# The second layer of a feed-forward stage as 7 block products instead of 8, with its weight sums made inside the stage

## What is computed

```python
n = layernorm(x3)                                  # rows of 512
h = gelu(n @ proj1.T + proj1_bias)                 # 4096 x 2048, tanh form
out = x3 + tanh(g_ffn) * (h @ proj2.T + proj2_bias)
```

## Time and profile before

| | |
|---|---|
| median of 3 runs | 3560.19 us (3558.64 to 3562.95) |
| the profiled execution | 3558.07 us, its span 3556.3 us |
| mean granted TensorE clock | 0.991 |
| TensorE matmuls, share of the span | 97% |
| VectorE, ScalarE, GpSimd | 65%, 52%, 45% |
| feed-forward stage | from 2879.9 us to the end, 676.4 us |

### The profile page before, as it was taken

How to read it: one execution, slowest core, us unless ns; L and a number is a source line. 1 busy time by engine, 2 the same in 40 slices (tenths; PEclk the granted TensorE clock), 3 DMA queues, 4 the chain that set the end, 5 groups by cost and what they waited for, 6 DMA issues and landing times. The chain is left out here.

```text
span 3556.3 us, 66541 instructions
## 1 busy us (share of the span) xinstructions
PE 3462.1 (97%) x22486; PEld 2994.5 (84%) x22486; DVE 2296.5 (65%) x5653; ACT 1863.4 (52%) x4821; POOL 1589.3 (45%) x1649
## 2 busy tenths in 40 slices
PE   8999999999999999799999997899999989999999
PEld 8999999999999998699999996567777668888887
DVE  6666666656666666577677777787777754545543
ACT  5555555554444444355555553877777753333332
POOL 4444444454444444455554453777777640202020
PEclk9999999999999999999999998999999999999999
DMA  4566666435666665476777774222222245344341
GB/s 167 186 237 236 237 238 237 162 102 184 241 229 229 226 236 168 165 281 245 257 250 256 263 262 143 67 85 65 66 64 71 74 125 163 107 131 124 113 130 48
DMA packets 431004, 610.97 MB, mean 172 GB/s; under 512 B 95265, under 2 KB 226466, under 8 KB 426658
## 3 DMA queue, kind: packets, MB, share of 16 engines
q1 hardware_dynamic: 330274, 394.91, 34.1%
q10 hardware_dynamic: 90208, 179.32, 13.7%
q0 software_dynamic: 10272, 33.63, 2.8%
HBM read 339.34 MB, written 268.44 MB: 171 GB/s over the span
## 5 line engine op out<-in xcount | busy, mean ns | idle before, releaser
L848 POOL TENSOR_SCALAR a_prob<-a_prob,a_rinv 128x256 f32<-128x256 f32 x512 | 472.4, 934 | 766.5 <-DVE a_rinv L1072 766.1
L767 ACT ACTIVATE a_prob<-a_prob,a_low_bias 128x256 f32<-128x256 f32 x512 | 256.4, 502 | 496.8 <-DVE a_low_bias L1063 496.8
L1377 POOL TENSOR_TENSOR e_act_hi<-e_act_f,e_zeros 128x256 fp32r<-128x256 f32 x128 | 181.8, 1420 | 310.5 <-DVE e_act_f L1592 310.5
L527 PE MATMUL a_pj<-a_xt,in_hi 128*128 128x256 f32 x1024 | 309.5, 302 | 0.1
L1391 PE MATMUL e_gb<-e_xt_hi,in_hi 128*128 128x256 f32 x1024 | 291.5, 285 | 3.0 <-DVE e_xt_lo L1571 3.0
L1393 PE MATMUL e_gb<-e_xt_hi,in_lo 128*128 128x256 f32 x1024 | 290.7, 284 | 0.0
L1392 PE MATMUL e_gb<-e_xt_lo,in_hi 128*128 128x256 f32 x1024 | 290.6, 284 | 0.0
L2961 DVE TENSOR_TENSOR raw_in<-turned,raw_in 128x512 f32<-128x512 f32 x224 | 151.9, 690 | 212.5 <-PE turned L2677 209.7
L529 PE MATMUL a_pj<-a_xt,in_lo 128*128 128x256 f32 x1024 | 288.8, 282 | 0.0
L528 PE MATMUL a_pj<-a_xt,in_hi 128*128 128x256 f32 x1024 | 288.5, 282 | 0.0
L902 DVE TENSOR_TENSOR a_ot_lo<-a_avb,a_ot_hi 128x256 fp32r<-128x256 f32 x256 | 108.3, 423 | 256.6 <-ACT a_ot_hi L776 256.6
(11 more groups left out here) (476 smaller groups left out, 11312.9 us busy)
## 6 DMA issues: line engine op xcount, KB each, us to landing
raw_in<-in_w_gate SPq DMA_DIRECT2D x39, 2048.0 KB, 8.6
x_sorted<-a_spare ACTq DMA_DIRECT2D x42, 1792.0 KB, 6.5
y_sorted<-a_spare ACTq DMA_DIRECT2D x42, 1792.0 KB, 8.6
raw_out<-in_w_out SPq DMA_DIRECT2D x40, 1024.0 KB, 5.5
in_hi<-w_ops SPq DMA_DIRECT2D x224, 128.0 KB, 2.3
in_lo<-w_ops SPq DMA_DIRECT2D x224, 128.0 KB, 2.4
xt_rows<-a_xt SPq DMA_DIRECT2D x16, 1024.0 KB, 5.5
a_xt<-xt_rows SPq DMA_DIRECT2D x16, 1024.0 KB, 6.1
```

Of the source, the lines that this page charges most:

```text
L527: nc.tensor.matmul(out, a_hi, b_hi, start=start, stop=False)
L767: e = nc.scalar.activation(prob[:, u % 4, t], prob[:, u % 4, t], ACT.Exp, bias=low_bias[:, u % 2, t:t + 1], scale=-1.0, accum_out=rsum[:, ...
L848: p = nc.gpsimd.tensor_scalar(prob[:, u % 4, t], prob[:, u % 4, t], rinv[:, u % 2, t:t + 1], None, ALU.mult)
```

## The change

The second layer is done as 7 block products as well, and its weights come through the same ring as the first layer's.

- In the pair, the hidden values of both chunks are kept (`h_kept` has room for 32 tiles), and the second layer is a 2 x 2 block product: hidden tiles 0 to 7 and 8 to 15 by chunk 0 and 1, weights by the halves of the 2048 hidden values and of the 512 outputs. `P1` to `P7` are 7 products of 8 steps each, so 56 steps a pair (`LAYER`); a step (`second`) is 12 matmuls with 256 moving columns. All steps of the second layer stand behind all products of the first.
- The sums of the hidden tiles that `P7`, `P5`, `P6` and `P3` need are made on POOL (`h_sum`), 32 of 128x512 a pair. Their hi and lo are made as before, 56 a pair, in 4 slots.
- The products leave in half banks of `ob`. DVE adds them to the rows of the two chunks (`take`, `outputs`), and what three of the blocks share is kept in `both` and added by POOL (`add_both`).
- The weights' sums `w2_ops` are made in the first pair, in 16 units. A unit: SP loads 4 blocks of `w2` of 128x128 (`load_unit`, 2 DMAs), POOL makes the 4 sums (`unit_sums`), ACT the highs (`unit_high`, 128x384 and 128x512), DVE the lows (`unit_low`), SP stores them to DRAM (`store_unit`, 4 DMAs of 384 and 512 runs of 512 bytes). There are rooms for 3 units. `UNITS` says with which step `j` of the first layer a unit is split.
- The ring has 16 places; 8 are filled in the stage before. `load_op` brings 56 operands of the first layer and 56 of the second for each pair, two DMAs of 128 KB each.
- All 7 sums of the rows of the next pair are awaited before its first product. The root of the layer norm is done for both chunks at once.
- `split_ahead`, `low_ahead`, `load_w2` and `split` go, and the attention stage no longer waits on ACT for its last stores.

```diff
-    RING = 8
+    RING, READY = 16, 8
@@ gated_normed_attention
-                if past in (-5, -4):
-                    split_ahead(past + 5)
...
-            for bb in range(2):
-                act.wait_ge(x_stored[bb], 16 * B + 32)
@@ feed_forward
+    UNITS = ((0, 1), (2, 3, 4), (5, 6, 7), (8, 9), (10, 11), (12, 13), (14, 15), ())
+    ROOMS, SLOTS = 3, 4
...
@@ SP
+            def load_unit(k):
+                j, half = divmod(k, 2)
+                b = unit_room(k)
+                raws = unit_rooms(k)[0].rearrange("p (a n) -> p a n", n=P)
+                if k >= ROOMS:
+                    sp.wait_ge(unit_kept[b], 64 * (k // ROOMS))
+                for a, cols in enumerate((D // 2, 0)):
+                    at = cols + half * P
+                    sp.dma_start(raws[:, 2 * a:2 * a + 2], w2[:, j:HC:JC, at:at + P]).then_inc(unit_loaded[b], 16)
+
+            def store_unit(k):
+                j, half = divmod(k, 2)
+                b = unit_room(k)
+                sp.wait_ge(unit_lod, 2 * k + 2)
+                to = w2_ops.rearrange("o j p h n -> p o j h n")[:, :, j, :, half * P:(half + 1) * P]
+                for ops, (los, his) in zip((slice(0, 3), slice(3, 7)), unit_ops(k)):
+                    for h, of in enumerate((his.bitcast(F32), los)):
+                        sp.dma_start(to[:, ops, h], of.rearrange("p (o n) -> p o n", n=P)).then_inc(unit_kept[b], 16)
+
+            for k in range(ROOMS):
+                load_unit(k)
+            for n in range(READY, RING):
+                load_op(n)
...
+            unit_at = [N * j + at for j, units in enumerate(UNITS) for at, _ in zip((3, 5, 6), units)]
+            store_at = [min(at + 3, second_op(0, 0, JC - 1) - RING - 1) for at in unit_at]
+            for n in range(RING, ALL):
+                p, at = divmod(n - RING, 2 * LAYER)
+                if p == 0:
+                    for k in range(2 * JC):
+                        if at == store_at[k]:
+                            store_unit(k)
+                        if at == store_at[k] + 2 and k + ROOMS < 2 * JC:
+                            load_unit(k + ROOMS)
...
+                load_op(n)
@@ PE
+            def second(p, q, j):
+                n, m = second_op(p, q, j), LAYER * p + JC * q + j
...
+                pe.wait_ge(ring_loaded[n % RING], ring_full(n))
+                pe.wait_ge(h_lod, m + 1)
...
+                for t in range(TC):
+                    mm = three(out[:, t // 2, t % 2], h_hi[m % SLOTS][:, t * P:(t + 1) * P], h_lo[m % SLOTS][:, t * P:(t + 1) * P], hi, lo, ...)
...
+            for p in range(PAIRS):
+                for j in range(JC):
+                    for i in range(N):
+                        first(p, j, i)
+                for s in range(LAYER):
+                    second(p, s // JC, s % JC)
@@ ACT, hidden(p, j)
+                gelu_of(0)
...
+                if p == 0:
+                    for k in UNITS[j][:1]:
+                        unit_high(k)
+                gelu_of(1)
...
+                gelu_of(2)
+                gelu_of(3)
+                if p == 0:
+                    for k in UNITS[j][1:]:
+                        unit_high(k)
@@ POOL
+            for k in range(2 * JC):
+                unit_sums(k)
             pool.wait_ge(bias_done, 1)
             residual(0)
...
+                if more:
+                    root(p)
+                for j in range(JC):
+                    h_sum(p, P7, j)
@@ DVE, early(p, j), which stands between additions 2 and 3
+                if p == 0:
+                    for k in UNITS[j][:1]:
+                        unit_low(k)
+                if p + 1 < PAIRS:
+                    if j in (3, 4):
+                        statistics(p, j - 3, (0, 1))
+                    if j == 5:
+                        aggregate(p)
+                    if j == 6:
+                        normalize(p, 0, (0, 1))
```

More of the change, by code:

```diff
@@ L1935, in _ @@
             sp.wait_ge(dca_ready, 4)
-            for n in range(ahead.RING):
+            for n in range(ahead.READY):
                 j, op = divmod(n, len(ahead.ORDER))
@@ L1945, in _ @@
             sp.dma_start(ahead.x_first, x_out[0:2 * S, :].rearrange("(t p) d -> p t d", p=P)).then_inc(ff_x_loaded[0], 16)
[L1946 to L1950, removed]
+            sp.wait_ge(ring_loaded, 32 * ahead.READY)
         @block.tensor
@@ L2869, in _ @@
-                if p + 1 < PAIRS:
-                    hidden(p + 1, 0)
+                for s in range(SLOTS, LAYER):
+                    high(p, s)
+                    if more:
+                        if s in (6, 8, 10, 12):
+                            take(p, (s - 6) // 2)
+                        for i, at in ((B22, 21), (T1, 25), (T2, 29), (T4, 37), (T3, 43)):
+                            if s in (at, at + 2):
+                                op_high(p + 1, i, (s - at) // 2)
         @block.gpsimd
@@ L2963, in hidden, with late, add @@
+            def late(p, j):
+                if j == JC - 1:
+                    h_low(p, 2)
+                    h_low(p, 3)
+                if p == 0:
+                    for k in UNITS[j][1:]:
+                        unit_low(k)
+                if p + 1 < PAIRS:
+                    if j in (3, 4):
+                        statistics(p, j - 3, (2, 3))
+                    if j == 6:
+                        normalize(p, 0, (2, 3))
             def hidden(p, j):
                 g = JC * p + j
+                def add(to, i, more):
+                    V.tensor_tensor(to, lw[:, BANK[i]], more, ALU.add).then_inc(added, 1)
@@ L3063, in _ @@
-                if more:
-                    hidden(p + 1, 0)
-                out(2 * p + 1)
+                    if p == j == 0:
+                        bias()
+                for s in range(SLOTS, LAYER):
+                    h_low(p, s)
+                    outputs(p, s)
+                    if more:
+                        if s in (4, 6, 8, 10):
+                            normalize(p, 1, ((s - 4) // 2,))
+                        for i, at in ((T1, 20), (T2, 24), (T4, 32), (T3, 38)):
+                            if s in (at, at + 2):
+                                op_sum(p + 1, i, (s - at) // 2)
+                        for i, at in ((B22, 28), (B11, 42), (B21, 46), (T2, 50)):
+                            if s in (at, at + 2):
+                                low_op(p + 1, i, (s - at) // 2)
@@ L3066, in feed_forward @@
+                last_output(p)
     clear(nc, used)
```

806 lines of the change are left out of this document (426 added, 380 removed).

## The result

The changed kernel takes 3635.73 us, the median of 4 runs (3635.04 to 3636.47), where the kernel before takes 3560.5 beside it: 1.0214 times as long, 95% interval 1.0202 to 1.0227. It is slower by 75 us; the prediction said by 23.

A forecast was written before the change was run, and what follows sets the result against it. TensorE, with matmuls in flight for 97% of the span, was taken to bound the kernel. Terms -25.6 - 1.6 - 1.5 + 48 + 2 + 1.5 = +22.8 us on 3558.07 gave 3580.9, as median 3583 us; range 3563 to 3607.

The forecast's parts named there:

- The second layer itself: Second layers: 2688 matmuls of 256 columns replace 1536 of 512, 322.6 us for 348.2: -25.6 us.
- the start: Feed-forward's start: no wait for ACT's last stores, -1.6 us; `w2` splits near the attention's end go, -1.5 us.
- The first pair's first layer: Pair 0's first layer: making 16 units beside the products delays its end from t = 84.8 to 133: +48 us.
- in bytes it is more: 107.5 us: Pair 0's first layer: 31.6 MB up to unit 15's load at 294 GB/s take longer than the issues' 97 us.
- 0.52 us an issue: SP's queue in pair 0's first layer: 187 issues back to back up to unit 15's load, 97 us.
- bound from above, +65: Pair 0's first layer: if unit stores ran at 227 GB/s, the term would be about +65 us.
- issues bind and bytes do not: Rival for pair 0's first layer: only SP's issues count, +33 us, kernel 3560 to 3567 us; chance 0.07.
- DVE beside POOL: Second layers: DVE's lows with two SBUF operands slow beside POOL, 0 to +8 us over four pairs, taken as +1.5.
- The sharing of SBUF: Rival: POOL and DVE sharing SBUF binds in all four pairs, +8 us or more, up to 3608 us; chance 0.12.
- Units that stay behind the products: Rival for pair 0's first layer: loads keep ahead, only the root's some 5 us show, about 3537 us; chance 0.11.
- waits of TensorE for `h_lod` in later pairs: Sign in the second layers of later pairs: such waits for DVE's lows would show the prediction wrong.
- The clock: Block 7 of pair 0's first layer: TensorE at its lower clock after long idling, about +2 us (0 to +4).

The follow-up runs named there:

- e16: Changed kernel without making the units and without POOL's sums of hidden tiles, and with `add_both` on DVE: 3530.65 us, ratio 0.9914.
- e7: Changed kernel with the units' stores cut to 64 of 128 partitions, as many DMA issues: 3631.30 us, ratio 1.0184.
- e9: Changed kernel with the 64 stores of the units issued by ACT in place of SP: 3631.55 us, ratio 1.0200.
- e10: Changed kernel with the units' stores both cut to 64 of 128 partitions and issued by ACT: 3623.01 us, ratio 1.0177.
- e8: Changed kernel with 52 of 56 DVE lows of hidden tiles in the last pair taking one operand from PSUM: 3631.21 us, ratio 1.0195.
- e1: Changed kernel without POOL's 32 sums of hidden tiles a pair, products reading the plain tiles: 3607.73 us, ratio 1.0132.

## Why the prediction was wrong, point by point

**The second layer itself, the start, -28.7 us: right.** Matmuls of 256 columns are 0.12 us apart. Alone the two terms give 3530.65 us (e16), where 3560.2 - 28.7 is 3531.5. Of the start, -3.1, the traces can't say as much: it is 2.6 us sooner in the changed kernel (2877.3 for 2879.9), 1.2 in e16 (2878.7), and over all the traces with the new start it lies between 2872.9 and 2882.4. That the sum comes out to a microsecond is in part luck. The formula of the Trainium skill that the prediction sets against the trace (TensorE: Matmul & The Clock Gate, section Back-to-back issue gap) is given there for an isolated matmul, and the section itself says that it is too low for a stream with weight loads at few columns and too high at many; here the trace is above it at both widths.

**The first pair's first layer, +48 us: right in its mechanism, mis-sized in its prices.** The span of the layer is 144.5 us for 133 forecast. Blocks 1 to 7 start, counted from 2877.3, at t = 19.1, 29.3, 54.1, 75.5, 89.7, 102.5 and 132.9, for 20, 31, 50, 70, 83, 95 and 123 forecast: the lag grows from block 3 on. It is all there when unit 15 comes: its operands were to be in SBUF at t = 111, and POOL starts on them at 122.8. From there on root, normalization, addition and seven products take 21.7 us, where 22 were forecast. The step that failed is "in bytes it is more: 107.5 us", together with pricing SP at 0.52 us an issue and then setting it aside. The bytes were counted right: 31.3 MB move in the 119.5 us up to unit 15's load, for 31.6 forecast. The rate was wrong: 294 GB/s was read from 2 us at the end of a burst, and over the whole way it is 262. The issue's price was wrong as well, 0.59 us in the mean, and near 1 us for the two behind four stores, so the issues take 111 us, and 8.3 us of waits and gaps of the in-order queue come on top. That a queue and engines that are both 0.93 full give less than either alone fits e7, e9 and e10, but it is argued. The prediction's bound from above, +65, comes to +60 by its own numbers (11.9 MB of stores at 227 in place of 294 GB/s are 12 us more). That is near the 59.7 measured, but no run shows that the stores are the part that goes slower. The rival "issues bind and bytes do not" was to give +33 us, and e7, where fewer bytes with as many issues take 7 us off, speaks against it.

**DVE beside POOL, +1.5 us: wrong by 44 us.** This is the step that put the time out of the range. It failed twice. The takes were counted at 0.74 us, the price of a tile of 512 elements; they have 1024 and take 1.27 (the earlier trace rows had no such form), 5.3 us more per pair. That alone would have been covered: e16 keeps all these takes and has TensorE's pace. The other is the price of the meeting. The earlier trace rows was read as a surcharge of 0.56 us at most on 32 lows. It is a lock: a DVE instruction with two operands in SBUF waits until POOL's is over, and the other way round. Then the two lists add up. An estimate from the runs for pair 1's second layer: POOL 30 x 1.3 for the sums (two of the 32 stand before it), 3 x 2.4 for `add_both` (its length in the last pair of e8, beside lows with an operand in PSUM) and 6 x 1.3 for its lows, 54.0 us; DVE 64 instructions with two SBUF operands at 0.60 from start to start, and 4 normalizations at 0.54, 40.6 us. That is 94.6 us for one lock in a layer of 84, and the layer took 95.1. So near an agreement is luck: in the trace POOL or such a DVE instruction is at work for 87.0 us of it, so the count is some 8 us too high. With the sums and `add_both` on DVE the same count is 7.8 + 40.6 + 19.2 + 3.8 = 71.4 us, the trace has 71.3, and the layer took 87.9, near TensorE's pace.

**The rivals.** The sharing of SBUF was named, with 0.12, and had the right engines, the right lines and the wrong size: +8 us or more for what is 44. Units that stay behind the products did not happen. The forecast's own warning sign, waits of TensorE for `h_lod` in later pairs, is in the trace (6.8 us in pair 1).

**The clock, +2 us.** In block 7 matmuls start 0.43 us apart at first, at the lower clock (0.64 granted from 3000 to 3020); the block takes 11.6 us where 10.5 and the 2 were forecast. About right. The clock was also down in the blocks before (0.87 granted from 2900 to 2980), which the term left out; what that cost isn't separated.

**The sum.** -2.6 for the start, -25.6, +59.7 for pair 0's first layer (144.5 - 84.8), +45.7: +77.2, for 76.9 in the span.

## What to carry to other kernels

Before work is moved to POOL, count per stretch all that POOL does with operands in SBUF and all that DVE does with two operands in SBUF, and add the two: here they ran nearly one after the other, and a normalization with one operand in SBUF belonged to the sum too. An operand in PSUM takes a DVE instruction out of that sum, and an addition of 0.6 us on DVE can be cheaper than the same of 1.3 us on an idle POOL. Where one queue brings loads and stores, work out its issues and its bytes both, and take neither price from a short burst of loads alone: here the two came within a tenth of each other by such prices, both prices were higher in the long run, and the time was longer than either.

## What the runs showed of the hardware

- A DVE low of 128x512 with two SBUF operands takes 0.68 to 0.69 us alone, and so does one with an operand in PSUM beside POOL's work (e8). With both in SBUF most take 1.2 to 1.8 beside POOL's additions of 512 elements and 2.4 to 2.9 where they meet those of 1024. A normalization with one SBUF operand, 0.54 us alone (e1), takes 1.51 in the mean beside POOL. POOL pays too: 1.29 us for a sum that takes 1.76 under the lock, and 7.3 in the mean for a low behind an unbroken list of DVE's.
- With loads and stores on SP's queue alone the engines moved 262 GB/s at a share of 0.93, with the stores on ACT's queue 304 GB/s.
- Most issues on SP's queue hold it for 0.47 to 0.53 us, and the two ring loads behind four stores of 192 to 256 KB for 0.96 in the mean. With stores of half the size (e7) the longest between 2940 and 2965 is 0.63. Where the stores are issued by ACT (e9), 22 of the 102 ring loads on SP's queue still hold it for over 0.8 us.
